# One kernel of two layers: in the first layer's step loop, TensorE multiplies weights and values ahead of the first banks of exponents and scores

## The chip, the core and the metric

The kernel runs on one core of a Trainium2 chip. A core has five engines with their own instruction queues: TensorE (PE; its weight loads are PEld), VectorE (DVE), ScalarE (ACT), GpSimd (POOL) and SyncE (SP, which issues the DMAs here). They meet through semaphores only. Matrix products land in PSUM, which has 8 banks of 128 partitions x 512 fp32 values; TensorE may write a bank again once the engine that reads it has signalled. The metric is the device time of one execution in microseconds, the median of several.

## The reference

Two transformer layers over x of shape 4 x 512 x 512, fp32. Each is an attention and a feed-forward part, each with a LayerNorm ahead of and behind it and a residual:

```python
x = x + _layernorm(_L0_attn_ref(_layernorm(x, axis=-1), L0_attn_Wq, L0_attn_Wkv, L0_attn_Wo), axis=-1)
x = x + _layernorm(_L0_ffn_ref(_layernorm(x, axis=-1), L0_ffn_q_scales, L0_ffn_q_vals, L0_ffn_bias), axis=-1)
x = x + _layernorm(_L1_attn_ref(...), axis=-1)
x = x + _layernorm(_L1_ffn_ref(...), axis=-1)
```

The change lies in the first attention: 32 heads of 16 columns, one key and value head for all, a linear position bias and a causal mask.

```python
scores = jnp.einsum('bqhd,bkd->bhqk', q, k) * scale
scores = jnp.where(causal[None, None], scores + bias[None], -jnp.inf)
attn = jax.nn.softmax(scores, axis=-1)
out = jnp.einsum('bhqk,bkd->bqhd', attn, v).reshape(b, s, h)
return out @ Wo
```

The first feed-forward part is one product with dequantized weights and a bias. The second layer (grouped attention with rotary positions, then a gated octonion feed-forward) isn't touched.

## The kernel before

Every fp32 operand of a product is split into two fp16 tensors, `hi` and `lo`, and three products (hi x hi, lo x hi, hi x lo) are added in PSUM.

The first layer (`layer0`) is one loop of steps, n from -6 to 73, written out once for each engine. A step works on pairs of heads; there are 64 pairs (4 batches x 16), and a pair passes through several steps:

- Step n: the scores of pair n (`scores`), in five banks s0 to s4, only for their row maxima. VectorE reduces each bank (`maximise`, L1074 for banks 0 and 1, L1076 for 2 and 3, L1079 for 4). The maxima of four pairs are joined, transposed, and put back by DMA as rows of `q_stack`.
- Step n: the exponents of pair n - 6 (`exponents`), transposed, with maxima subtracted, in five banks x0 to x4. ScalarE takes the exponential of each bank (`exponential`, L872). GpSimd casts them to hi in three pieces (`weights_hi`, L564) and makes the last piece's lo (L566); VectorE makes the other lo halves, two pieces, one step later (`weights_lo`, L1088).
- Step n: the product of weights and values of pair n - 8 (`weigh_values`, 60 matmuls of 17 columns into one bank, L687 and L690). ScalarE copies the heads out (`copy_heads`, L879), VectorE takes reciprocals, GpSimd normalises.
- Between these, `others(n)` puts in queries (q), keys (K), values (V), the products of output (y) and feed-forward (f), and transposes of normed rows (n1, n2, n3) and heads (o). The first of a step's others stands between bank 2 and 3, a large one in two halves about bank 3; the rest and the transpose of maxima (m) stand between bank 3 and 4.

The banks are in three groups (`groups`): three for scores, two for exponents, three for the rest, each used in turn. Before a bank is filled, `take` waits until the filling that used it before has been emptied. So the third-last filling of the last group (PV, others, m) must be emptied before PV can start; a transpose is emptied by VectorE's lo half (`lo4`, L1019), after ScalarE's hi half (L823).

The queues are strict in the order written. ScalarE's steps also carry the row norms (L863) between the exponentials in some steps (of 16: steps 0, 4, 8, 10 and 14, where a batch has them). VectorE's step: lo half 0 of pair n - 7, maxima 0 and 1, lo half 1, maxima 2 and 3, first other, statistics, maximum 4, other others, reciprocals.

Of the kernel before, what the change touches and what calls it, by code (L numbers as in the profile page):

```python
# [213 lines left out]
def layer0(nc, A, W0, C, K0, N1, xT, x2_dram):  # L214
# [9 lines left out]
    with ExitStack() as stack:  # L224
# [138 lines left out]
        def others(n):  # L363
            out = []
            g, r = divmod(n + 5, GP)
            if r == 0 and 0 <= g < NG:
                out.append(("q", g))
            if at(n, FRONT["K"]) is not None:
                out.append(("K", at(n, FRONT["K"])))
            for kind in ("y", "f"):  # L370
                out += [(kind, b, t) for t in range(TT) for b in range(B)
                        if n == PAIRS * b + offset(kind, b, t) and has(kind, b)]
            if at(n, FRONT["V"]) is not None:
                out.append(("V", at(n, FRONT["V"])))
            for kind, when in (("n1", FRONT["n1"]), ("n2", BACK["n2"]), ("n3", BACK["n3"])):
                for i, w in enumerate(when):
                    b = at(n, w)
                    if b is not None and has(kind, b):
                        out += [(kind, b, 2 * i), (kind, b, 2 * i + 1)]
            out += [("o", b, t) for t in range(TT) for b in range(B) if n == PAIRS * b + offset("o", b, t)]  # L380
            return out
# [78 lines left out]
        with nc.Block() as block:  # L460
# [158 lines left out]
            def _(pe):  # L619
# [29 lines left out]
                def scores(p, i):  # L649
                    g, pp = p // GP, p % GP  # L650
                    if (pp, i) == (0, 0):
                        pe.wait_ge(s_qs[g % 2], 16 * 6 * (g // 2 + 1))
                        pe.wait_ge(s_kr, 4 * (g // GP) + 2)
                    out = take(("s", p, i))
                    for e, t, c in PARTS[i]:
                        w = P * (t + 1)
                        pe.matmul(out[:, c:c + w], qs[:, g % GP, pp, t * P:(t + 1) * P], kz[:, g // GP % 2, e, 0:w],  # L657
                                  start=True, stop=False)
                        ins = pe.matmul(out[:, c + w - P:c + w], far[:, :], tri[:, :], start=False, stop=True)
                    ins.then_inc(s_sf, 1)  # L660

                def exponents(p, i):
                    g, pp = p // GP, p % GP
                    if (pp, i) == (0, 0):
                        pe.wait_ge(s_mr[g % 2], 16 * 4 * (g // 2 + 1))
                        pe.wait_ge(s_kr, 4 * (g // GP) + 4)
                    out = take(("x", p, i))
                    for e, j, c in XPARTS[i]:
                        pe.matmul(out[:, c:c + S - j * P], ks[:, g // GP % 2, e, j * P:(j + 1) * P],  # L669
                                  qs[:, g % GP, pp, j * P:S], start=True, stop=False)  # L670
                        ins = pe.matmul(out[:, c:c + P], far[:, :], trit[:, :], start=False, stop=True)  # L671
                    ins.then_inc(s_ef, 1)
# [22 lines left out]
                def turn_maxima(g):  # L695
                    out = take(("m", g))
                    pe.wait_ge(s_mx, g + 1)
                    pe.transpose(out[:, 0:P], mx[:, g % 2, :], C["ident"][:, :]).then_inc(s_mf, 1)
# [70 lines left out]
                def turn(n, *which):  # L769
                    for i in which:  # L770
                        if 0 <= n - X_LAG < NP:
                            exponents(n - X_LAG, i)
                        if 0 <= n < NP:
                            scores(n, i)

                for n in STEPS:
                    extra = others(n)
                    if n == 0:
                        pe.wait_ge(s_sc, 1)
                    turn(n, 0, 1)  # L780
                    if 0 <= n - V_LAG < NP:
                        weigh_values(n - V_LAG)
                    turn(n, 2)
                    split = bool(extra) and extra[0][0] in ("K", "q", "y", "f")
                    for u in extra[:1]:
                        if split:
                            half(u, 0)
                        else:
                            fill(u)
                    turn(n, 3)  # L790
                    for u in extra[:1]:
                        if split:
                            half(u, 1)
                    if n % GP == 0 and 0 <= n // GP - 1 < NG:
                        turn_maxima(n // GP - 1)
                    for u in extra[1:]:
                        fill(u)
                    turn(n, 4)
# [1987 lines left out]
```

## Time and profile before

| | |
|---|---|
| median of 3 runs | 2198.66 us (2198.51 to 2199.24) |
| the profiled execution's own time | 2201.45 us |
| its span, first to last instruction | 2199.3 us |
| mean granted TensorE clock | 0.978 |
| busy TensorE / VectorE / ScalarE / GpSimd | 2061.8 / 1755.3 / 1387.8 / 950.2 us |
| first layer's step loop | about 62 to 640 us; x banks from 95 to 577 us |

The page gives the engine, the line in the kernel, the tile names, and the microseconds of each. A wait is put down to the engine that released it last. Matmuls overlap, so a matmul's duration is longer than its distance to the next one; in the timelines the distance between starts counts. "PEclk" is the share of TensorE's full clock that was granted.

### The profile page before, as it was taken

The page shows a single profiled execution, that of the slowest core. Times are in us where ns is not written, and L with a number is a line of the kernel's source. Part 1 is how long each engine was busy: PE and PEld are TensorE (multiplying, and loading weights), DVE is VectorE, ACT ScalarE, POOL GpSimd, SP SyncE. Part 2 cuts the span into 40 slices and gives each one's busy share as a digit, 9 for nine tenths or more (in the row PEclk, how much of TensorE's full clock was granted, in tenths as well). Part 3 has the DMA queues.
Part 4 walks back from the last instruction along what each step waited for, and adds up shares of the span by engine and source line. Part 5 has one row for each costly group of instructions (what it writes and reads, how often), then busy time and mean ns, then how long its engine had stood idle before and what let it go on. Part 6 is the DMA issues. An engine that isn't in the chain of part 4 may idle for free. (4 is left out here: it accounts for less than half of the span.)

```text
span 2199.3 us, 48564 instructions
## 1 busy us (share of the span) xinstructions
PE 2061.8 (94%) x18563; PEld 1248.1 (57%) x18563; DVE 1755.3 (80%) x3692; ACT 1387.8 (63%) x3037; POOL 950.2 (43%) x902
## 2 busy tenths in 40 slices
PE   8798999898878899999999999999999999888998
PEld 3466666666434556656566565666666665534443
DVE  5799899998766787778878778777877877967665
ACT  3466665666456777777777777767777876661221
POOL 0188798879743323233333332332333323253221
PEclk9899999999879999999999999999999999999999
DMA  6110101101122453354354354444354443420001
GB/s 240 47 36 17 55 17 48 36 18 41 44 96 55 92 101 76 71 95 92 63 97 90 67 93 89 71 91 92 63 99 80 73 89 76 98 71 27 32 20 39
DMA packets 390214, 153.81 MB, mean 70 GB/s; under 512 B 358544, under 2 KB 369424, under 8 KB 387936
## 3 DMA queue, kind: packets, MB, share of 16 engines
q1 hardware_dynamic: 389984, 150.71, 31.5%
q8 instruction: 148, 2.42, 0.5%
q14 instruction: 82, 0.67, 0.1%
HBM read 48.69 MB, written 11.53 MB: 27 GB/s over the span
## 5 line engine op out<-in xcount | busy, mean ns | idle before, releaser
L1899 POOL TENSOR_TENSOR q_in_sbuf<-q_in_sbuf,sinq 128x512 f32<-128x512 f32 x128 | 162.6, 1271 | 720.1 <-ACT q_in_sbuf L2031 598.5
L2043 ACT ACTIVATE xp<-xp,nm 128x128 f32<-128x128 f32 (+3 forms) x512 | 281.3, 550 | 199.0 <-DVE nm L2126 199.0
L1925 PE MATMUL bank<-xT_hi,weights_and_hi 128*128 128x512 f16 x1280 | 383.0, 381 | 7.0 <-DVE yacc L2141 3.8
L872 ACT ACTIVATE weights_and_hi<-bank,unit 128x512 f32<-128x512 f32 x320 | 213.4, 687 | 152.3 <-PE bank L671 149.6
L2008 ACT ACTIVATE probs_hi<-xp,rl 128x128 f16<-128x128 f32 (+3 forms) x512 | 245.1, 550 | 68.2 <-DVE rl L2146 64.4
L2095 DVE SCALAR_TENSOR_TENSOR probs_lo<-xp,rl,probs_hi 128x128 f16<-128x128 f32 (+3 forms) x512 | 282.4, 612 | 0.0
L2103 DVE TENSOR_TENSOR q1T_lo<-qf,q1T_hi 128x512 f16<-128x512 f32 x128 | 88.4, 691 | 222.8 <-ACT q1T_hi L2022 222.8
L2126 DVE CUSTOM_DVE_ANT_0 xp<-bank,mask,cs 128x128 f32<-128x128 f32 (+3 forms) x512 | 250.3, 545 | 0.0
L1925 PE MATMUL bank<-xT_lo,weights_and_hi 128*128 128x512 f16 x640 | 243.6, 381 | 0.0
L564 POOL CAST weights_and_hi<-weights_and_hi 128x1024 f16<-128x1024 f32 (+1 forms) x192 | 198.4, 1053 | 85.9 <-ACT weights_and_hi L872 85.4
L1925 PE MATMUL bank<-p1T_hi,v_hi 128*128 128x128 f16 x1280 | 221.0, 219 | 2.6 <-DMA p1T_lo<-probs_lo 2.6
L1925 PE MATMUL bank<-p1T_hi,v_lo 128*128 128x128 f16 x1280 | 221.0, 219 | 0.0
L1925 PE MATMUL bank<-p1T_lo,v_hi 128*128 128x128 f16 x1280 | 221.0, 219 | 0.0
L1925 PEld LDWEIGHTS bank<-xT_hi,weights_and_hi 128*128 128x128 f16 x1280 | 124.7, 98 | 161.0 <-issue 15.0
L1906 POOL TENSOR_TENSOR qf<-q_in_sbuf,t 128x512 f32<-128x512 f32 x160 | 203.9, 1274 | 12.7 <-POOL q_in_sbuf L1899 0.2
L1925 PE MATMUL bank<-wo_hi,o1T_hi 128*128 128x512 f16 x512 | 195.0, 381 | 6.3 <-DVE wo_lo L2185 4.7
L1925 PE MATMUL bank<-wo_hi,o1T_lo 128*128 128x512 f16 x512 | 195.1, 381 | 0.0
L1925 PE MATMUL bank<-wo_lo,o1T_hi 128*128 128x512 f16 x512 | 195.1, 381 | 0.0
L1088 DVE TENSOR_TENSOR weights_lo<-weights_and_hi 128x1024 f16<-128x1024 f32 x128 | 181.4, 1421 | 6.0 <-POOL weights_and_hi L564 6.0
L657 PE MATMUL bank<-k_stack_max,q_stack 128*128 128x512 f16 (+3 forms) x512 | 137.2, 310 | 32.2 <-DVE mx L1076 12.9
L1925 PE MATMUL bank<-kT_hi,q1T_hi 128*128 128x128 f16 (+3 forms) x512 | 148.1, 302 | 11.0 <-DVE q1T_lo L2103 8.3
L669 PE MATMUL bank<-q_stack,k_stack 128*128 128x512 f16 (+3 forms) x512 | 139.1, 313 | 17.2 <-ACT weights_and_hi L872 10.0
(311 smaller groups left out, 5498.2 us busy)
## 6 DMA issues: line engine op xcount, KB each, us to landing
weights_and_hi<-in_wq SPq DMA_DIRECT2D x8, 1024.0 KB, 6.0
raw_o<-in_wo SPq DMA_DIRECT2D x8, 1024.0 KB, 6.0
x_front<-in_x SPq DMA_DIRECT2D x5, 1024.0 KB, 6.1
q_stack<-q_hi SPq DMA_DIRECT2D x64, 64.0 KB, 2.6
wup<-in_wup SPq DMA_DIRECT2D x3, 1024.0 KB, 11.9
fused_scratch<-weights_and_hi SPq DMA_DIRECT2D x12, 256.0 KB, 2.5
xb<-in_x SPq DMA_DIRECT2D x3, 1024.0 KB, 5.2
x_scratch<-xb SPq DMA_DIRECT2D x3, 1024.0 KB, 4.3
```

The lines of the kernel that those rows point to most:

```text
L564: pool.tensor_copy(ph[0][:, p % 2, c0:c1, :], px[:, p % 2, c0:c1, :]).then_inc(s_wh, 1)
L657: pe.matmul(out[:, c:c + w], qs[:, g % GP, pp, t * P:(t + 1) * P], kz[:, g // GP % 2, e, 0:w], start=True, stop=False)
L669: pe.matmul(out[:, c:c + S - j * P], ks[:, g // GP % 2, e, j * P:(j + 1) * P], qs[:, g % GP, pp, j * P:S], start=True, stop=False)
L872: act.activation(px[:, p % 2, i, :], bank_of(("x", p, i))[:, :], ACT.Exp, scale=unit[:, 0:1]).then_inc(s_ed, 1)
L1088: dve.tensor_tensor(ph[1][:, p % 2, c, :], px[:, p % 2, c, :], ph[0][:, p % 2, c, :], ALU.subtract).then_inc(s_wl, 1)
L1899: pool.tensor_tensor(qs[:, i % 2, :], qs[:, i % 2, :], rope["sink" if u[0] == "k" else "sinq"][:, :], ALU.mult).then_inc(s_rot, 1)
L1906: pool.tensor_tensor(qf[:, i % 2, :], qs[:, i % 2, :], t2[:, i % 2, :], ALU.add).then_inc(s_qf, 1)
L1925: ins = pe.matmul(out, lhs(a), rhs(c), start=(first and i == 0), stop=(last and i == 2))
L2008: ins = act.activation(pr[0][:, m % 2, c], xp[:, m % 3, c], ACT.Copy, scale=rl[:, m % 3, t:t + 1])
L2043: ins = act.activation(x, x, ACT.Exp, scale=-1.0, bias=nm[:, m % 3, t:t + 1], accum_out=ls[:, m % 3, t:t + 1])
L2095: ins = dve.scalar_tensor_tensor(pr[1][:, m % 2, c], xp[:, m % 3, c], rl[:, m % 3, t:t + 1], pr[0][:, m % 2, c], ALU.mult, ALU.subtract)
L2126: ins = dve.tensor_tensor_reduce(out=xp[:, m % 3, TRI[t]:TRI[t] + w], in0=bank_of(("s", m, i))[:, col:col + w], in1=mask[:, S - w:S], scal ...
```

## The change

In TensorE's block, the call of `weigh_values` moves ahead of the banks 0 and 1 of exponents and scores. No other engine's code changes.

```diff
                     if n == 0:
                         pe.wait_ge(s_sc, 1)
-                    turn(n, 0, 1)
                     if 0 <= n - V_LAG < NP:
                         weigh_values(n - V_LAG)
-                    turn(n, 2)
+                    turn(n, 0, 1, 2)
                     split = bool(extra) and extra[0][0] in ("K", "q", "y", "f")
```

TensorE, head of step 26, before. The rows from `q_stack,k_stack` are exponents, those from `k_stack_max,q_stack` scores, those with `v` the product of pair 18; brackets name the semaphores waited for (`s_t_lo_out`: VectorE's lo halves of transposes):

```order
L657 MATMUL bank<-k_stack_max,q_stack 128x256
...
L669 MATMUL bank<-q_stack,k_stack 128x512 [waits s_exponentials,s_key_stacks_ready,s_maxima_stacked1]
...
L657 MATMUL bank<-k_stack_max,q_stack 128x512 [waits s_scores_maximised]
...
L669 MATMUL bank<-q_stack,k_stack 128x512 [waits s_exponentials]
...
L657 MATMUL bank<-k_stack_max,q_stack 128x512 [waits s_scores_maximised]
...
L687 MATMUL bank<-v,weights_and_hi 128x17 [waits s_last_weights_lo,s_weights_lo,s_t_lo_out]
...
L669 MATMUL bank<-q_stack,k_stack 128x384 [waits s_exponentials]
...
L657 MATMUL bank<-k_stack_max,q_stack 128x128 [waits s_scores_maximised]
```

The same place after:

```order
L657 MATMUL bank<-k_stack_max,q_stack 128x256 [waits s_scores_maximised]
...
L687 MATMUL bank<-v,weights_and_hi 128x17 [waits s_last_weights_lo,s_weights_lo,s_t_lo_out]
...
L669 MATMUL bank<-q_stack,k_stack 128x512 [waits s_exponentials,s_key_stacks_ready,s_maxima_stacked1]
...
L657 MATMUL bank<-k_stack_max,q_stack 128x512 [waits s_scores_maximised]
...
L669 MATMUL bank<-q_stack,k_stack 128x512 [waits s_exponentials]
...
L657 MATMUL bank<-k_stack_max,q_stack 128x512 [waits s_scores_maximised]
...
L669 MATMUL bank<-q_stack,k_stack 128x384 [waits s_exponentials]
```

The product's group of 60 matmuls, with its three waits, stands ahead of x0; x0, s0, x1, s1 and x2 follow in their old order.

TensorE, head of step 69, before (exponents of pair 63, product of pair 61; there are no scores any more):

```order
L669 MATMUL bank<-q_stack,k_stack 128x256 [waits s_exponentials]
...
L669 MATMUL bank<-q_stack,k_stack 128x512 [waits s_exponentials]
...
L669 MATMUL bank<-q_stack,k_stack 128x512 [waits s_exponentials]
...
L687 MATMUL bank<-v,weights_and_hi 128x17 [waits s_last_weights_lo,s_weights_lo,s_pv_out]
...
L669 MATMUL bank<-q_stack,k_stack 128x384 [waits s_exponentials]
...
L639 MATMUL bank<-wf_hi,back_T_hi 128x512 [waits s_t_lo_out]
```

The same place after:

```order
L669 MATMUL bank<-q_stack,k_stack 128x256 [waits s_exponentials]
...
L687 MATMUL bank<-v,weights_and_hi 128x17 [waits s_last_weights_lo,s_weights_lo,s_pv_out]
...
L669 MATMUL bank<-q_stack,k_stack 128x512 [waits s_exponentials]
...
L669 MATMUL bank<-q_stack,k_stack 128x512 [waits s_exponentials]
...
L669 MATMUL bank<-q_stack,k_stack 128x384 [waits s_exponentials]
...
L639 MATMUL bank<-wf_hi,back_T_hi 128x512 [waits s_t_lo_out]
```

There x0 and x1 of the last pair moved behind the product, which waits for GpSimd's lo half (`s_last_weights_lo`).

## Rows read from the trace of the kernel before

**Rows 1.** Busy time (x instructions) by engine, PEclk, DMA share, GB/s, by stretch.
```profile
100.00:230.00 130.00, 117.22 (x1908) 85.21 (x1906) 128.14 (x197) 84.52 (x153) 113.36 (x102) 1.00 0.08 25
...
530.00:590.00 60.00, 48.81 (x693) 33.45 (x692) 43.88 (x58) 33.65 (x63) 51.22 (x48) 0.80 0.16 45
```

**Rows 2.** What VectorE waited for, 230 to 530 us: us in total, times, longest.
```profile
DVE mx L1079 <- PE bank L659: 8.6, 6, 1.8
DVE st L1005 <- ACT ya L853: 4.2, 7, 1.3
```

**Rows 3.** What TensorE's weight loads waited for, 100 to 530 us.
```profile
PEld bank L657 <- DVE mx L1076: 23.2, 38, 2.3
PEld bank L669 <- ACT weights_and_hi L872: 19.3, 41, 1.4
...
PEld bank L687 <- DVE front_T_lo L1019: 1.6, 4, 0.5
```

**Rows 4.** TensorE's timeline, step 26: start us, us, instruction, [idle before <-releaser].
```profile
227.59 0.38 PE L669 MATMUL bank<-q_stack,k_stack 128*128 128x512 f16 x1
...
229.24 0.21 PE L687 MATMUL bank<-v,weights_and_hi 128*128 128x17 f16 x2 [0.15 <-DVE front_T_lo L1019]
...
230.76 0.32 PE L669 MATMUL bank<-q_stack,k_stack 128*128 128x384 f16 x1
```

**Rows 5.** Timeline of VectorE, steps 26 and 27.
```profile
228.51 0.68 DVE L1019 TENSOR_TENSOR front_T_lo<-bank,front_T_hi 128x512 f16<-128x512 f32 x1
...
245.61 0.69 DVE L1079 TENSOR_REDUCE mx<-bank 128x2 f32<-128x512 f32 x1 [1.77 <-PE bank L659]
```

**Rows 6.** Timeline of TensorE, step 11.
```profile
127.58 0.39 PE L657 MATMUL bank<-k_stack_max,q_stack 128*128 128x512 f16 x1 [0.90 <-DVE mx L1076]
...
127.86 0.38 PE L669 MATMUL bank<-q_stack,k_stack 128*128 128x512 f16 x1
...
129.97 0.32 PE L669 MATMUL bank<-q_stack,k_stack 128*128 128x384 f16 x1
```

**Rows 7.** Timeline of VectorE, step 11.
```profile
125.71 1.21 DVE L1088 TENSOR_TENSOR weights_lo<-weights_and_hi 128x1024 f16<-128x1024 f32 x1
```

**Rows 8.** Timeline of ScalarE, step 11.
```profile
128.33 0.69 ACT L872 ACTIVATE weights_and_hi<-bank,unit 128x512 f32<-128x512 f32 x1 [0.87 <-PE bank L671]
```

**Rows 9.** Timeline of TensorE, step 59.
```profile
494.79 0.39 PE L669 MATMUL bank<-q_stack,k_stack 128*128 128x512 f16 x1 [0.85 <-ACT weights_and_hi L872]
...
496.86 0.32 PE L669 MATMUL bank<-q_stack,k_stack 128*128 128x384 f16 x1
```

**Rows 10.** Timeline of ScalarE, end of step 58 and head of step 59.
```profile
494.06 0.67 ACT L872 ACTIVATE weights_and_hi<-bank,unit 128x512 f32<-128x512 f32 x1
494.63 0.81 ACT L863 ACTIVATE yb<-yb,nb,rs 128x512 f32<-128x512 f32 x1
```

**Rows 11.** Busy time by engine, from step 55 on.
```profile
462.00:472.50 10.50, 10.50 (x124) 6.56 (x122) 8.28 (x13) 5.03 (x9) 5.15 (x5) 1.00 0.01 2
```

**Rows 12.** Timeline of TensorE, step 53.
```profile
447.52 0.21 PE L687 MATMUL bank<-v,weights_and_hi 128*128 128x17 f16 x2
```

**Rows 13.** Timeline of VectorE, steps 53 and 55.
```profile
446.79 0.68 DVE L1019 TENSOR_TENSOR back_T_lo<-bank,back_T_hi 128x512 f16<-128x512 f32 x1
...
472.31 0.69 DVE L1079 TENSOR_REDUCE mx<-bank 128x2 f32<-128x512 f32 x1 [1.78 <-PE bank L659]
```

**Rows 14.** Timeline of TensorE, step 69.
```profile
569.97 0.20 PE L687 MATMUL bank<-v,weights_and_hi 128*128 128x17 f16 x2 [0.41 <-POOL weights_lo L566]
```

**Rows 15.** Timeline of GpSimd, step 69.
```profile
567.81 2.01 POOL L566 TENSOR_TENSOR weights_lo<-weights_and_hi 128x512 f16<-128x512 f32 x1
```

**Rows 16.** Timeline of VectorE, step 69.
```profile
576.61 0.75 DVE L1060 SCALAR_TENSOR_TENSOR yb<-bank,gm,bias 128x512 f32<-128x512 f32 x1 [1.72 <-PE bank L639]
```

**Rows 17.** VectorE's lo half of the weights: count, shortest, median and longest in ns.
```profile
L1088 DVE TENSOR_TENSOR weights_lo<-weights_and_hi x128: 1165/1215/2316, 103.2 to 581.5; 128x1024 f16<-128x1024 f32 x128
```

**Rows 18.** Granted clock (PEclk, after POOL) in steps 34 and 35.
```profile
297.00:303.00 6.00, 5.93 (x85) 3.73 (x83) 5.86 (x14) 1.64 (x4) 5.92 (x7) 0.72 0.01 3
```

## The prediction

> **What bounds the kernel now.** I read the page's slices first, then the busy time by stretch, the waits of each engine, and last the timeline of single steps. The change touches only the step loop of the first layer, which puts its first exponent bank at 95 us and its last product of weights and values at 585 us. Between 100 and 230 us VectorE is busy 128.1 of 130 us [rows 1], which leaves 1.9 us for all its waits. Its own instructions set the pace there. Between 230 and 530 us it waits 19.7 us, of which 8.6 for scores from TensorE and 4.2 for ScalarE copies of output banks that TensorE fills late [rows 2], the rest mostly for such copies of queries, keys and transposes. In those places TensorE is the bound. Steps with an output or query product are TensorE's, the others VectorE's. TensorE waits often, mostly at the head of a step: 23.2 us for the maxima that free score banks, 19.3 for exponentials [rows 3]. For weights and values ("PV" below) it waits only 1.6 us, behind a lo half of a transposed tile [rows 3]. From 530 us GpSimd sets the pace, busy 51.2 of 60 us [rows 1].
>
> **What the change does to a step.** A step n fills x0 s0 x1 s1 PV x2 s2 x3 s3 x4 s4 (x: exponents, s: scores), with other products between. Now PV stands ahead of x0. Nothing is added or removed: 60 short matmuls move past four banks, 64 times. No DMA and no instruction of another engine moves. PV takes 1.52 us (229.24 to 230.76, rows 4), the four banks 0.28 us each when nothing is late (127.58 to 127.86, rows 6), 1.12 us together.
>
> PV needs three things. (a) The weights of pair n-8: VectorE's second lo half, which it computes just ahead of the maximum that s0 waits for. In step 11 that half ends at 125.71 + 1.21 = 126.92, while s0 goes at 127.58 [rows 6, 7]. (b) GpSimd's last lo half of the pair: by the timeline of every step from 8 to 63 it is done before the head, but for step 35, where it is 0.06 us late. (c) A bank of the group of three that is filled for PV, transposes and products in turn. After a step with three other fillings that bank is the first of them, and it is emptied late in VectorE's step. In step 26 its lo half ends at 228.51 + 0.68 = 229.19 and PV starts at 229.24; x0, s0, x1, s1 had run meanwhile from 227.59 [rows 4, 5]. I read (c) from the timeline of each step: it already holds PV back in steps 9, 25, 26, 37, 42 and 53, and it comes 1.15 us after the head in steps 41 and 49.
>
> **Price A, where (c) ends last.** PV starts as before, but four banks now stand behind it, so x2 comes at least 1.12 us later. ScalarE adds to that: an exponential starts 0.47 us after its bank's matmul (127.86 to 128.33), lasts 0.69, and the bank is taken 0.06 us later (494.06 + 0.67 to 494.79): 1.22 us from x0 to x2 [rows 6, 8 to 10]. I take 1.22. The ends are 0 (the wait is passed on to nothing) and 1.22 plus ScalarE's queue behind the late exponentials, 0.8 us for one row norm (494.63, rows 10).
> - Step 26: x2 moves from 230.76 to 231.98 and TensorE is dense on to 245.6, where VectorE waits 1.77 us for scores [rows 4, 5]. But step 27 wins 0.2 at x1, and steps 28 to 31, still TensorE's, 0.6 together. 1.2 - 0.2 - 0.6 = +0.4.
> - Step 53: PV starts at 447.52, right after back_T_lo (446.79 + 0.68). TensorE is busy 10.50 of the last 10.5 us up to VectorE's next long wait, 1.78 us at 472.31 [rows 11 to 13], and as dense in the 12 us ahead of these. All of it arrives: +1.25.
> - Steps 37 and 38: the lateness meets a score wait in step 39 (0.66 us of gap), so about +0.4. Step 42: +1.2, of which step 43 gives 1.0 back: +0.2.
> - Steps 9, 25, 41, 49: the third score bank waits for VectorE's maximum anyway, and the maxima of banks 3 and 4 start 1.4 to 1.8 us after these could. Zero; the cover is VectorE's dense queue.
> - The tail: PV of pair 61 (the last is 63) waits for GpSimd's lo half (567.81 + 2.01 = 569.82) and starts at 569.97; x2 follows 1.5 us later, then products for which VectorE waits 1.72 us at 576.61 [rows 14 to 16]. x0 and x1 now stand between: +1.2.
>
> **Price B, ScalarE.** In steps 24, 36, 40 and 52, whose row norms sit between the exponentials, exponentials 0 and 1 come about 1.3 us later and push copies of transposes. VectorE reads one 0.3 us too early in perhaps three: +0.9.
>
> **Gain C, where the head waited for something else.**
> - Steps bound by the score bank: in step 11 PV can run from 126.97 to 128.48, x2 comes at 129.70 instead of 129.97 [rows 6, 7]. That is 0.27 us, and it counts only where VectorE waits afterwards: three such steps in the dense stretch, -0.8 (at most the 1.9 us of idle time there, rows 1).
> - Step 59: x1 waited until 494.79 for the last exponential of the step before. With PV at 493.23 to 494.74, x2 is bound by ScalarE's norm (to 495.44) and exponential 0, about 496.06 instead of 496.86: -0.8, and step 58 gives 0.3 more [rows 9, 10]. Together -1.1.
> - Step 62, -0.4. In other steps (18, 22, 33, 34, 47) the head's wait is covered too, but the next one, for VectorE's maximum or ScalarE, ends as before: zero.
>
> **The sum.** 0.4 + 1.25 + 0.4 + 0.2 + 1.2 + 0.9 - 0.8 - 1.1 - 0.4 = +2.05 us. The profiled span of 2199.3 would become 2201.3. Its run took 2201.45 us, 2.8 above the median of 2198.66, so I add the 2.05 to the median: **2200.7 us**.
>
> **A second look at GpSimd.** One lo half of VectorE takes 1.165 to 2.316 us, 128 of them [rows 17]; their total on the page's line is 181.4 us, mean 1.42, so 32 us lie above the shortest. The long ones overlap GpSimd's two-input operations. Later first exponentials could shift GpSimd's casts, but it starts a pair's first cast 1.3 us or more after its exponential in nearly all steps, and the later casts hang on x3 and x4. I take 0, with 3 us to either side (a tenth of the 32). The Trainium skill (SBUF — State Buffer, "Who interferes with whom") says that a VectorE instruction with two SBUF inputs and a GpSimd instruction that reads SBUF contend, and that whichever starts first blocks the other. The trace agrees on the lengthening; by that rule a shift of either sign could cost as much as it saves, and the sum would stay.
>
> **Rivals.**
> 1. *PV at the head blocks the banks behind it everywhere (slower).* Against my zeros: all eight steps of price A pay 1.22 us, and the tail. 9 x 1.22 = 11.0, less C's 2.3, plus B's 0.9: +9.6, 2208. It decides once the maxima's slack of 1.4 to 1.8 us after a late s3 is used up, for instance by the ScalarE queue's 0.8 us on top of 1.22 (2.0 in all). For: TensorE is in order. Against: VectorE is dense in these steps. A half of it is +5, 2204.
> 2. *The head waits are simply filled (faster).* TensorE waits 42.5 us for maxima and exponentials [rows 3]; if a third of VectorE's 19.7 us went, with the tail's price halved: about -6, 2193. Against: (a) opens only 0.66 us ahead of s0, and (c) is a wait that filling can't shorten.
> 3. *TensorE's clock.* After two waits of 1.9 and 1.5 us in steps 34 and 35 the granted clock was 0.72 over six us [rows 18], that is partly at 1.2 instead of 2.4 GHz; 28% of six us is 1.7 us lost. There are three such drops between 290 and 525 us. Moving PV closes some gaps (step 35's, ahead of s0) and joins others into one of up to 2.1 us (step 37). One drop more or fewer: 2202.4 or 2199.0. The Trainium skill (TensorE: Matmul & The Clock Gate, "What's actually happening") says that the default state is throttled and activity releases it, which speaks for a drop more wherever a joined gap lengthens. The profile has gaps of 1.5 us without a drop, so the sum leaves it out.
> 4. *No change* (PV hides wholly): 2198.7, inside my range.
>
> **Chances.** What a measurement here can tell from no change is about 0.2%, 4.4 us: 2194.3 to 2203.1. My forecast with 3 and 4: 0.62, of which 0.06 ends above 2203.1 and 0.01 below 2194.3. Rival 1, whole or half: 0.25, of which 0.05 still lies within. Rival 2: 0.13, of which 0.04 within. Faster 0.10, same 0.64, slower 0.26. Range: 2195.5 (half of rival 2, or 3 us from GpSimd) to 2207 (most of rival 1).
>
> **What would show it.** In the new profile: PV starts at the head in most steps, and after a front_T_lo or back_T_lo in steps 26, 37, 42 and 53 at an unchanged distance from it; TensorE waits of 0.3 us or less for exponentials at x2; VectorE's waits between 230 and 530 us near 20 us; the stage's last PV near 586 to 587 us; then everything shifted by one constant. I am wrong if the step loop to 530 us is over 3 us longer or shorter, if maxima of banks 3 or 4 are waited for in steps 9, 25, 41 and 49, or if the mean of VectorE's lo half moves by more than 0.03 us.

## The result, and the profile after

| kernel | median | lowest to highest | executions |
|---|---|---|---|
| before | 2199.64 us | 2198.40 to 2202.01 | 13 |
| after | 2204.44 us | 2203.02 to 2209.69 | 13 |

By the medians the change costs 4.8 us. The ratio, which is estimated from all executions, is 1.0028, with a 95% interval of 1.0020 to 1.0035, which is 6.2 us (4.4 to 7.7). It is not the quotient of the medians, here and below; the two agree within the interval. The forecast was 2200.7, range 2195.5 to 2207.0. The sign and the range held; the size was too small by more than half. The profiled execution of after is its longest, 2209.69 us with a span of 2207.6. The same kernel, run and profiled once more, gave 2206.14 us with a span of 2204.0. I call it "after, second" and read terms from it where a typical execution is wanted. Lines behind 779 have a number one lower than before. A "fall" of the clock is a stretch in which PEclk is 0.50 instead of 1.00.

Busy time by stretch of after, columns as in [rows 1]. The second row is the whole stretch from 230 to 530 us, the last one the 7 us behind step 26's wait:

```profile
100.00:230.00 130.00, 116.91 (x1891) 84.43 (x1890) 128.18 (x196) 82.94 (x149) 111.03 (x102) 0.99 0.08 25
230.00:530.00 300.00, 277.04 (x3901) 190.08 (x3898) 274.40 (x443) 177.44 (x314) 239.13 (x223) 0.95 0.11 34
530.00:590.00 60.00, 47.97 (x701) 33.57 (x698) 41.94 (x62) 39.65 (x71) 55.22 (x52) 0.76 0.07 20
229.00:236.00 7.00, 6.86 (x90) 4.59 (x91) 6.69 (x10) 2.76 (x6) 3.60 (x4) 0.76 0.08 25
```

The same stretches of before, those that [rows 1] lack:

```profile
230.00:530.00 300.00, 276.58 (x4008) 191.29 (x4005) 278.87 (x457) 183.07 (x325) 248.47 (x230) 0.98 0.11 34
229.00:236.00 7.00, 6.85 (x102) 4.63 (x100) 7.00 (x12) 4.02 (x8) 4.81 (x4) 1.00 0.10 31
```

From 230 to 530 us TensorE is as busy as before (277.0 to 276.6 us) and does fewer instructions (3901 to 4008). Its granted clock is 0.95 instead of 0.98. VectorE is busy 4.5 us less, since it does less in the same time. That TensorE is as busy as before is easy to misread: a slow TensorE looks as busy as a fast one, and only PEclk and the counts tell them apart.

What VectorE waited for, 230 to 530 us of after (us in total, times, longest), against [rows 2]:

```profile
DVE mx L1078 <- PE bank L659: 8.7, 6, 1.8
DVE st L1004 <- ACT ya L852: 4.8, 7, 1.3
DVE q_lo L1050 <- ACT q_hi L846: 3.9, 5, 1.2
DVE k_placed L1027 <- ACT k_hi L833: 1.2, 1, 1.2
DVE mx L1073 <- PE bank L659: 1.2, 4, 0.5
DVE mx L1075 <- PE bank L659: 1.2, 2, 0.8
```

In all VectorE waits 23.7 us there, 19.7 before.

What TensorE's weight loads waited for, 100 to 530 us of after, against [rows 3]:

```profile
PEld bank L669 <- ACT weights_and_hi L871: 19.0, 52, 1.7
PEld bank L657 <- DVE mx L1073: 13.7, 15, 3.3
PEld bank L687 <- issue: 12.2, 15, 1.9
...
PEld bank L687 <- DVE front_T_lo L1018: 4.6, 4, 1.5
PEld bank L687 <- DVE back_T_lo L1018: 2.9, 2, 1.4
PEld bank L687 <- DVE m_lo L1097: 2.5, 2, 1.3
```

Before has this row besides those in [rows 3]:

```profile
PEld bank L657 <- DVE mx L1074: 14.0, 22, 2.3
```

The waits for maxima of banks 0 to 3 shrank from 23.2 + 14.0 us to 13.7. The product of weights and values (L687) took the waiting over: where before had 1.6 us for a front_T_lo and 0.7 for a back_T_lo, after has 4.6 + 2.9 + 2.5 us for lo halves of the rest group, in pieces of up to 1.5 us, and 12.2 us for no releaser that the profile shows.

TensorE in step 26 of after (start us, us, instruction, [idle before <-releaser]), against [rows 4]:

```profile
229.14 0.21 PE L687 MATMUL bank<-v,weights_and_hi 128*128 128x17 f16 x2 [1.15 <-DVE front_T_lo L1018]
...
230.66 0.42 PE L669 MATMUL bank<-q_stack,k_stack 128*128 128x512 f16 x1
...
231.51 0.63 PE L669 MATMUL bank<-q_stack,k_stack 128*128 128x512 f16 x1
...
232.58 0.53 PE L669 MATMUL bank<-q_stack,k_stack 128*128 128x384 f16 x1
```

PV starts behind front_T_lo as before, now after one wait of 1.15 us. x0, x1 and x2 follow at 230.66, 231.51 and 232.58. The second 128x512 matmul lasts 0.63 us where one of before lasts 0.38, and x1 to x2 takes 1.07 us where two banks took 0.56. From the granted clock, 0.76 over the seven microseconds, half the clock (1.2 instead of 2.4 GHz) was granted for a part of them. x2 moved by 1.82 us, and VectorE's first maximum of step 27 lies 2.71 us more behind before's than that of step 26.

Step 9 has the same form; the forecast had it at zero. TensorE's row there in after:

```profile
114.23 0.21 PE L687 MATMUL bank<-v,weights_and_hi 128*128 128x17 f16 x2 [1.25 <-DVE front_T_lo L1018]
```

And in before:

```profile
115.52 0.21 PE L687 MATMUL bank<-v,weights_and_hi 128*128 128x17 f16 x2 [0.15 <-DVE front_T_lo L1019]
```

In the tail this profile agrees with the forecast. GpSimd's last lo half, PV and VectorE's wait in step 69 of after, against [rows 14 to 16]:

```profile
577.22 2.01 POOL L566 TENSOR_TENSOR weights_lo<-weights_and_hi 128x512 f16<-128x512 f32 x1
```
```profile
579.37 0.20 PE L687 MATMUL bank<-v,weights_and_hi 128*128 128x17 f16 x2 [0.49 <-POOL weights_lo L566]
```
```profile
587.29 0.75 DVE L1059 SCALAR_TENSOR_TENSOR yb<-bank,gm,bias 128x512 f32<-128x512 f32 x1 [3.00 <-PE bank L639]
```

PV comes 9.40 us later than before (579.37 to 569.97), VectorE's feed-forward row 10.68 (587.29 to 576.61): the tail adds 1.28 us. VectorE's lo half, against [rows 17], kept its mean (181.5 us in 128, 1.42 each):

```profile
L1087 DVE TENSOR_TENSOR weights_lo<-weights_and_hi x128: 1164/1234/2307, 101.9 to 592.2; 128x1024 f16<-128x1024 f32 x128
```

**How the traces are compared.** The start of VectorE's first maximum in each step is a good ruler, since all kernels have it 64 times. Its shift against before grows or shrinks at the steps where time is lost or won. For after, second:

| first maximum of step | change of the shift, us | edit or cause |
|---|---|---|
| 9 and 10 | +0.39, +1.06 | steps 8 and 9 |
| 12, 14, 17, 20 | -0.13, -0.15, -0.14, -0.13 | gain C |
| 25, 41, 53 | +0.24, +0.30, +0.24 | price B |
| 27, then to 32 | +2.71, then -0.34 | step 26 |
| 38 | +1.33 | step 37 |
| 43, 44 | +0.96, -0.28 | step 42, given back in 43 |
| 49, 50 | +0.93, -0.55 | steps 48 and 49 |
| 54, 55 | +0.82, +0.28 | step 53 |
| 59, 60, 61 | -0.15, -1.24, +0.68 | steps 58 and 59 |

From step 8 to 63 all terms make +7.3 us (ahead of step 8 the executions already differ by up to 1.3 us, without any edit), and the tail adds 1.3. In the first profile it is +10.6 us.

What the loop and its tail lose doesn't arrive whole. The next layer's first ScalarE copy of queries starts 10.8 us later than before in the first profile and 7.4 us later in the second, but the executions end 8.3 and 4.7 us later. The second layer from there on, with no instruction changed, took 2.5 and 2.7 us less than in the profile of before, and in the profiles of the experiments 0.1 to 3.7 us less. So a shift of a few microseconds in one profile isn't the change of a median; terms are read from the first maxima, costs from the medians.

### The profile page after: what moved, and what is told of

The parts are those of the page before. It is cut to its first block and busy times, and to the rows that moved or that the text cites. A ratio compares the mean times of both kernels' runs of the same rounds, so it can differ in the third digit from the quotient of the medians.

```text
span 2207.6 us, 48564 instructions
## 1 busy us (share of the span) xinstructions
PE 2070.8 (94%) x18563; PEld 1253.3 (57%) x18563; DVE 1758.0 (80%) x3692; ACT 1389.1 (63%) x3037; POOL 946.7 (43%) x902
## 5 line engine op out<-in xcount | busy, mean ns | idle before, releaser
L1087 DVE TENSOR_TENSOR weights_lo<-weights_and_hi 128x1024 f16<-128x1024 f32 x128 | 181.5, 1422 | 5.1 <-POOL weights_and_hi L564 5.1
L1924 PE MATMUL bank<-kT_lo,q1T_hi 128*128 128x128 f16 (+3 forms) x512 | 154.5, 302 | 0.0
## 6 DMA issues: line engine op xcount, KB each, us to landing
wup<-in_wup SPq DMA_DIRECT2D x3, 1024.0 KB, 11.9
```

Of the source, the lines that this page charges most:

```text
L1087: dve.tensor_tensor(ph[1][:, p % 2, c, :], px[:, p % 2, c, :], ph[0][:, p % 2, c, :], ALU.subtract).then_inc(s_wl, 1)
L1924: ins = pe.matmul(out, lhs(a), rhs(c), start=(first and i == 0), stop=(last and i == 2))
```

## The experiments

All ran against the kernel before on the same chip; times are medians with the lowest and highest. "Late steps" are the eight in which the bank of the rest group ends last: 9, 25, 26, 37, 41, 42, 49 and 53. In the texts on record theory L says that the late bank, with the clock, makes the cost; theory S, that ScalarE's queue (price B) makes it all over the loop.

**After, second.** No edit.

> The changed kernel again, on the chip of the three others. Theory L (late bank: the loss comes from the eight steps 9, 25, 26, 37, 41, 42, 49 and 53, whose PV waits for a bank, and from the granted clock that falls in that joined wait): +4 to +6 us over before, with two groups of runs, some 3 us apart, by how many times the clock falls; in the profile at least five falls of the clock before 535 us, against three before the change. Theory S (ScalarE: exponentials 0 and 1 come later in every step and delay its copies): the same +4 to +6, but the clock's falls are a by-product and don't decide a run's time.

2206.14 us (2204.96 to 2208.03), before 2198.24; ratio 1.0034 (1.0021 to 1.0047). That is +7.9 us by the medians, above the +4 to +6 of both theories, though the interval reaches down to 4.6. The five executions don't form two groups. The falls did come: seven of them between 100 and 535 us, against three in before. Its step loop loses time at the same places as the first profile, to 0.1 us each up to step 51. From there the first profile lost 3.1 us more, with further falls of the clock at 435 and 456 us.

**The new order except in the late steps and the tail.** `turn(n, 0, 1)` stands ahead of `weigh_values` where `head` is false, `turn(n, 2)` behind it:

```diff
+                    head = n < NP and n not in (9, 25, 26, 37, 41, 42, 49, 53)
+                    if not head:
+                        turn(n, 0, 1)
                     if 0 <= n - V_LAG < NP:
                         weigh_values(n - V_LAG)
-                    turn(n, 0, 1, 2)
+                    turn(n, 2) if not head else turn(n, 0, 1, 2)
```

> PV at the head in all steps from 8 to 63 but the eight with a late bank (9, 25, 26, 37, 41, 42, 49, 53) and the steps from 64 on, which keep the old order. Theory L: only the gains of price C and price B are left, +0.9 - 2.3 us, so before -1.4, between -2.5 and 0. Theory S: nearly all steps are still changed, so +3 to +5 us. The tail (steps from 64 on) is out too: were it the tail alone, this would be -1.4 as well, and the run with the eight steps alone would be 0.

2198.62 us (2195.61 to 2201.48), ratio 1.0001 (0.9992 to 1.0010). The whole cost is gone, so the late steps and the tail make it. Theory S asked for +3 to +5 us and is out, since the interval ends at +2.2. The forecast gain of 1.4 us did not show.

**The new order in the late steps only.**

Against the edit above:

```diff
-                    head = n < NP and n not in (9, 25, 26, 37, 41, 42, 49, 53)
+                    head = n in (9, 25, 26, 37, 41, 42, 49, 53)
```

> PV at the head only in the eight steps with a late bank, the old order in all others. Theory L: prices of these steps without the gains elsewhere, which feed on the same waits: +5 to +8 us, above the changed kernel. Theory S: 8 of 56 steps, under +1 us. Tail alone: 0.

2209.24 us (2207.01 to 2211.40), ratio 1.0046 (1.0034 to 1.0059). By the medians (+11.0 us, more than the +5 to +8 expected) eight steps cost more than the whole change does, and the rest of the change gives some back; the intervals of the two ratios overlap.

**Late steps kept busy.** The order of after, and in the late steps four spare products into x0's bank, which x0 overwrites, run while PV's bank is waited for:

```diff
+                    if n in (9, 25, 26, 37, 41, 42, 49, 53):
+                        spare = take(("x", n - X_LAG, 0))
+                        for _ in range(4):
+                            pe.matmul(spare[:, :], far[:, :], posr[:, :], start=True, stop=True)
```

> The changed kernel, with four matmuls of 128 x 512 ahead of PV in each of the eight steps, into the free bank that x0 takes next and overwrites (0.86 us of work in a wait of 1.2 to 1.9 us). If the granted clock is part of the loss (theory L): faster than the changed kernel by 1 to 3 us, that is before +2 to +3, with the runs closer together, and one or two falls of the clock fewer in each place; the 1.22 us a step of banks behind PV stay. If the clock is no part: the same as the changed kernel or up to 1 us slower.

2201.69 us (2198.98 to 2204.50), ratio 1.0014 (1.0005 to 1.0023). TensorE has more work, and the time is 4.4 us less than after, second, on the same chip. The slowest of these eleven executions is faster than the fastest of those five. The text on record expected them closer together; they spread over 5.5 us, the five over 3.1. Step 26 on TensorE: the spare products, PV, x0 and x2.

```profile
227.09 1.03 PE L783 MATMUL bank<-position_rows,far 128*128 128x512 f16 x4
...
228.41 0.21 PE L687 MATMUL bank<-v,weights_and_hi 128*128 128x17 f16 x2 [0.29 <-DVE front_T_lo L1022]
...
229.93 0.38 PE L669 MATMUL bank<-q_stack,k_stack 128*128 128x512 f16 x1
...
231.20 0.34 PE L669 MATMUL bank<-q_stack,k_stack 128*128 128x384 f16 x1
```

The granted clock behind it, in the same kernel:

```profile
228.00:235.00 7.00, 6.69 (x97) 4.33 (x97) 7.00 (x11) 3.50 (x7) 4.41 (x5) 1.00 0.10 31
```

The idle piece is 0.29 us instead of 1.15, the clock stays at 1.00, and x0 to x2 takes 1.27 us. So the order alone delays x2 by what the forecast said, and the rest of step 26 went away with the fall behind it. The first maxima tell the same (us):

| change of the shift at | 10 | 27 | 38 | 43 |
|---|---|---|---|---|
| after, second | +1.06 | +2.71 | +1.33 | +0.96 |
| kept busy | +0.46 | +1.25 | +0.35 | +0.44 |
| clock's part | 0.60 | 1.46 | 0.98 | 0.52 |

Together 3.6 us. After, second has falls at 114.7, 230.8, 316.1 and 353.7 us, right behind the waits for PV's bank in steps 9, 26, 37 and 41; with TensorE kept busy none of the four is left. The last stands behind step 41's wait of 1.04 us, so the 0.52 us at step 43 is not step 42's own:

```profile
353.20 0.21 PE L687 MATMUL bank<-v,weights_and_hi 128*128 128x17 f16 x2 [1.04 <-DVE m_lo L1097]
```

**Four late steps.** `head = n in (26, 37, 42, 53)`.

> The order of before everywhere, but in steps 26, 37, 42 and 53 the product of weights and values stands ahead of x0. Theory L (late bank and clock): these four steps alone give +4 to +6 us against before. From the maxima of the kernel with the new order everywhere: 2.7 at step 26, 1.35 at 37, 0.95 at 42 and 0.8 to 2.6 at 53, less the 0.3 to 0.5 us that dense steps give back between them; the granted clock falls behind each of the four. Theory P (the prediction's price A as it was written, no clock): 0.4 + 0.4 + 0.2 + 1.25 = +2.2 us. If the cost sits in the sum of many steps instead: under +1.

2206.82 us (2205.99 to 2211.35), before 2199.65; ratio 1.0039 (1.0027 to 1.0052): +7.2 us by the medians, above both theories. Its first maxima rise by 2.43, 1.82, 1.92 and 1.07 us behind the four steps, and by 1.19 at step 36 and 1.50 at step 63, where no instruction changed. Behind step 35's old wait the clock now lost 3.4 us, in before 1.7. All kernels that have the old order and no spare products in steps 34 and 35 fit this: the four that lose 3.4 us there pay 1.19 or 1.20 us at step 36, the five that lose 1.7 or nothing pay nothing. Step 53's rise has no fall behind it.

**The other four.** `head = n in (9, 25, 41, 49)`.

> The order of before everywhere, but in steps 9, 25, 41 and 49 the product stands ahead of x0. The prediction said zero for these four: 0, within 0.5 us. The trace of the kernel after says otherwise for step 9: its first maximum came 1.47 us later, with a fall of the granted clock behind the joined wait, and steps 25 and 41 gave 0.25 to 0.3 each: +1.3 to +2.0 us for the four.

2203.62 us (2201.72 to 2207.71), ratio 1.0019 (1.0010 to 1.0028): +4.0 us, more than the +1.3 to +2.0 expected. The four steps themselves: +1.61 (step 9), +0.34 (25), +0.40 (41), and +0.51 and -0.52 about step 49. The rest are again unchanged places: +1.20 at step 36, +0.51 at 44, +1.56 and -0.51 at 52 and 53, +1.70 at 63.

**The tail alone.** `head = n >= NP`.

> The order of before in all steps up to 63, and the product ahead of x0 from step 64 on. The prediction's price for the tail: +1.2 us (+0.1 to +1.5 by the start of layer 1 in the kernels run so far), no shift of any maximum before 525 us. If the tail hides it: 0.

2199.64 us (2196.66 to 2202.79), ratio 1.0003 (0.9994 to 1.0012). No cost is measured, but the interval (-1.3 to +2.6 us) doesn't exclude the forecast +1.2. Its first maxima lie 0.1 to 0.5 us ahead of before's at every step. The next layer's first ScalarE copy of queries starts at 646.04 us, in before at 646.28. With the first maximum of step 63 0.44 us ahead, the tail adds 0.2 us. Over the same stretch the six kernels with the old tail and no spare products lie between -0.66 and +0.08, so the price is 0.1 to 0.9 us. From PV to the feed-forward row, the ruler that gave 1.28 in after, the tail alone adds 0.59.

**Spare products in the waits, in the order of before.** Six in step 61 ahead of s3, three in step 62 ahead of s0, and more ahead of PV in the last steps:

```diff
+                def spend(bank, count):
+                    for _ in range(count):
+                        pe.matmul(bank[:, :], far[:, :], posr[:, :], start=True, stop=True)
...
+                    if n in (67, 68, 69):
+                        spend(take(("pv", n - V_LAG)), 2 if n == 69 else 6)
...
-                    turn(n, 3)
+                    if n == 61:
+                        exponents(n - X_LAG, 3)
+                        spend(take(("x", n - X_LAG, 4)), 6)
+                        scores(n, 3)
+                    else:
+                        turn(n, 3)
```

> The order of before, with spare products of 128x512 (operands far and posr) put where TensorE waits anyway: six into x4's bank in step 61, three into x1's bank in step 62, six into the output bank of weights and values in steps 67 and 68, four and two in step 69. Each is overwritten by the first real product of its bank. If the granted clock falls in these waits and costs time (the clock part of theory L): -1 to -2.5 us against before. If the clock in the last steps of the stage decides nothing, or the spare products delay what stands behind them: 0 to +1 us.

2196.75 us (2194.61 to 2199.21), ratio 0.9988 (0.9979 to 0.9996): 2.9 us less than before by the medians, a little more than expected. The first maximum of step 63 gains 0.76 us on that of step 62.

**Four late steps kept busy.** The kernel with `head = n in (26, 37, 42, 53)`, and the four spare products in these steps:

```diff
                     if not head:
                         turn(n, 0, 1)
+                    else:
+                        spare = take(("x", n - X_LAG, 0))
+                        for _ in range(4):
+                            pe.matmul(spare[:, :], far[:, :], posr[:, :], start=True, stop=True)
```

> As the kernel with the product ahead of x0 in steps 26, 37, 42 and 53 only, but in these four steps four spare products of 128x512 run into x0's bank while the product's bank is waited for; x0 overwrites them. If the falls of the granted clock behind the joined waits are most of the +7.2 us that the four steps cost: +2 to +3.5 us against before (price A as the prediction had it is +2.25; the first maxima of the kernel with spare products in all late steps give 1.25 + 0.35 + 0.44 + 0.82 = 2.9). If the cost is the order of the banks alone: +6 to +8 us still.

2207.66 us (2202.96 to 2209.35), before 2199.29; ratio 1.0028 (1.0016 to 1.0041). The total is a miss: +8.4 us by the medians, by the interval 3.5 to 9.0, where the clock theory asked for 2 to 3.5. The spare products did not lower the +7.2 us of the same four steps without them, so this run doesn't bear the theory out as a whole. Two of the four steps did as expected: step 26 cost 1.25 instead of 2.43, step 42 cost 0.44 instead of 1.92. Step 53 cost 1.07 instead of 1.06; it had no fall to lose. In step 37 the spare products ran too early, PV still waited in one piece, and the cost stayed at 1.82 us:

```profile
314.48 0.21 PE L687 MATMUL bank<-v,weights_and_hi 128*128 128x17 f16 x2 [0.95 <-DVE back_T_lo L1025]
```

The kernel with all late steps kept busy waited 0.35 us there. In places where no instruction changed the profile pays another 1.20 (step 36), 1.49 (48) and 1.50 us (63).

**Ten chosen steps.** The order of before, PV ahead of x0 only where earlier kernels had won time:

```diff
+                    early = n in (11, 13, 16, 19, 27, 29, 31, 43, 58, 59)
+                    if early:
+                        weigh_values(n - V_LAG)
                     turn(n, 0, 1)
-                    if 0 <= n - V_LAG < NP:
+                    if not early and 0 <= n - V_LAG < NP:
```

> The order of before, with the product ahead of x0 only in steps 11, 13, 16, 19, 27, 29, 31, 43, 58 and 59, whose next first maximum came earlier in the kernels run so far: 0.10 to 0.16 us each in eight of them, 0.79 in step 43, 1.23 in step 59. Gains that add up: -3 us against before. If these gains come back as waits further down (GpSimd sets the pace from 530 us on): 0 to -1.

2198.50 us (2195.04 to 2200.63), ratio 0.9995 (0.9986 to 1.0004): -0.8 us by the medians, as the second of the two expectations had it. In its trace the gains are there: -0.11 to -0.17 in eight places, -0.78 at step 44, -1.24 at step 60. But it pays 1.19 us at step 36 and 1.63 at step 48, and step 61 takes 0.66 back.

**Ten chosen steps and the spare products of steps 61 to 69.** Both edits.

> The kernel with the product ahead of x0 in the ten chosen steps, and the spare products in steps 61, 62, 67, 68 and 69. The spare products alone gave -2.9 us. If both add: -4.5 to -6 us against before, the best of all. If the end of the stage is set by GpSimd and takes the chosen steps' gain back: -3, as with the spare products alone.

2197.42 us, ratio 0.9989 (0.9979 to 0.9998), with ten of eleven executions from 2192.36 to 2201.16: 1.9 us under before by the medians, less than either expectation, though the interval reaches to -4.6. The eleventh took 3502.65 us, with a mean granted clock of 0.556 against 0.98 in the others; it has no trace, and its cause is open. Up to step 60 this kernel and the one ahead have the same instructions in the same order. In the profiled executions their first maxima of step 54 still lie 3.7 us apart, 0.6 of it from ahead of step 8. The wait ahead of x1 in step 47 and the 7 us behind it in the kernel without spare products:

```profile
398.24 0.39 PE L669 MATMUL bank<-q_stack,k_stack 128*128 128x512 f16 x1 [1.03 <-ACT weights_and_hi L875]
```
```profile
399.00:406.00 7.00, 6.83 (x86) 4.20 (x83) 5.92 (x13) 4.80 (x9) 6.35 (x7) 0.76 0.47 152
```

The same in the kernel with them:

```profile
396.57 0.39 PE L669 MATMUL bank<-q_stack,k_stack 128*128 128x512 f16 x1 [1.03 <-ACT weights_and_hi L896]
```
```profile
397.00:404.00 7.00, 6.83 (x102) 5.01 (x100) 6.33 (x14) 5.82 (x11) 6.65 (x8) 1.00 0.52 152
```

The same instruction waits the same 1.03 us. In one execution TensorE then gets 0.76 of its clock and does 86 instructions, in the other 1.00 and 102. The waits of 1.77 and 1.36 us in steps 34 and 35 differ in the same way: behind them the granted clock over six us is 0.64 in the one and 1.00 in the other. So a wait of over a microsecond is a risk and not a fixed price. Nor is the length of the wait all that counts: before waits 1.57 and 2.00 us in one piece ahead of 414.6 and 432.0 us with no fall behind, after in step 41 1.04 us with one.

**More spare products.** As the kernel ahead, and also:

```diff
-                    if n == 62:
+                    if n in (35, 50, 51, 62):
                         exponents(n - X_LAG, 0)
-                        spend(take(("x", n - X_LAG, 1)), 3)
+                        spend(take(("x", n - X_LAG, 1)), {35: 4, 50: 4, 51: 5, 62: 3}[n])
                         scores(n, 0)
                         turn(n, 1)
+                    elif n == 47:
+                        turn(n, 0)
+                        spend(take(("pv", n - V_LAG)), 3)
+                        turn(n, 1)
...
-                    if n == 61:
+                    if n in (34, 61):
```

> The kernel with the ten chosen steps and the spare products of steps 61 to 69, and further spare products of 128x512 in the regular waits behind which the granted clock fell in some executions and not in others: six ahead of s3 in step 34, four ahead of s0 in step 35, three ahead of x1 in step 47, four ahead of s0 in step 50 and five in step 51. If these chance falls are what makes executions of one kernel differ by several us: no fall between 100 and 540 us, a first maximum of step 63 at -4 us or earlier, a median 4 to 6 us under before, and a spread of the executions under 4 us (7.8 us for before in the last comparison). If the falls there have little to do with the spread: -2 us as without these spare products, and the same spread.

2192.86 us (2192.03 to 2194.21), before 2197.95 (2194.82 to 2202.38); ratio 0.9977 (0.9967 to 0.9986). This is 5.1 us under before, the best of all, and its ten executions lie within 2.2 us, those of before within 7.6. All its numbers came as the first theory said. (The text above gives 7.8 us for the spread of before in the comparison ahead of this one; on record it is 9.8.) TensorE in steps 34 and 35, and the clock:

```profile
291.73 0.23 PE L657 MATMUL bank<-k_stack_max,q_stack 128*128 128x128 f16 x1 [0.48 <-DVE mx L1102]
...
293.40 1.04 PE L778 MATMUL bank<-position_rows,far 128*128 128x512 f16 x4 [0.24 <-ACT weights_and_hi L900]
```
```profile
100.00:540.00 440.00, 408.40 (x6125) 284.89 (x6124) 419.34 (x670) 280.16 (x501) 374.98 (x343) 1.00 0.10 33
```

**All kernels side by side.** "Clock lost" adds up what PEclk lacks to 1 in each microsecond from 100 to 540 us of the profiled execution; the shift is that of the first maximum of step 63 against before, and the last column leaves out what was there at step 8 already.

| kernel | clock lost, us | shift, us | from step 8 on |
|---|---|---|---|
| before | 5.4 | 0 | 0 |
| chosen steps and more spare products | 0.0 | -4.4 | -3.4 |
| chosen steps and spare products | 1.7 | -4.1 | -3.2 |
| order of before, spare products | 1.7 | -1.1 | -0.9 |
| tail alone | 3.4 | -0.4 | 0.0 |
| chosen steps | 10.3 | +0.3 | +0.5 |
| new order except in late steps | 10.5 | -0.3 | +0.9 |
| after, late steps kept busy | 6.8 | +1.4 | +2.6 |
| after, second | 15.4 | +6.1 | +7.3 |
| four other late steps | 15.4 | +6.7 | +7.0 |
| four late steps kept busy | 13.6 | +8.3 | +9.5 |
| after | 18.8 | +9.3 | +10.6 |
| late steps only | 11.9 | +9.5 | +9.9 |
| four late steps | 15.4 | +10.6 | +10.8 |

The two go together but are not proportional. I read this as falls that count only where TensorE sets the pace. Before itself loses 1.7 us at 298 us and the tail-only kernel does not, with no difference in the maxima behind it. The first two kernels below before lie close together because the profile of the one with one fall is of its fastest execution, 2192.36 us; by the medians they are 5.1 and 1.9 us under before.

## Why the prediction was right or wrong

- **The range** held, but not for the sum's reasons: it reached to 2207 for rival 1, and no term of the sum was the clock.
- **What bounds the kernel** held in the main: VectorE's waits for the maxima of bank 4 stay what they were (8.7 to 8.6 us), its waits in all grew from 19.7 to 23.7, and the cost sits where TensorE sets the pace.
- **Price A, as an order.** Right in size but for step 26. x0 to x2 was put at 1.22 us; with TensorE kept busy it was 1.27. Without the clock's part step 26 costs 1.25 less the 0.35 that steps 27 to 31 give back (forecast +0.4, so 0.5 too little), step 37 +0.35 (+0.4), step 42 +0.44 - 0.27 (+0.2), step 53 +0.82 (+1.25). The next 0.28, at step 55, can't be laid to step 53: the kernel that keeps its old order has it too.
- **The step that failed** is rival 3's last sentence, "so the sum leaves it out". I had seen that the change joins gaps, and took the falls of the clock as one more or one fewer. There were some eight more (1.7 us of full clock each): the clock lost from 100 to 540 us rose from 5.4 to 18.8 us, in after, second to 15.4, six more. Their part at four places is 3.6 us by the kernel kept busy, more than the 2.75 us between the forecast of +2.05 and the measured +4.8. In the loop alone the forecast's terms add up to +0.85 from step 8 on; after, second has +7.3, with TensorE kept busy +2.6. So most of what was missing went away with the falls, and 1.8 us is order that the terms had too small.
- **Why its argument failed.** It was that the profile has gaps of 1.5 us without a drop. That is true and proves only that a gap is no certain drop. I had counted the three drops, but not how many gaps of over a microsecond the change would add. In after PV's bank makes one of 1.04 to 1.25 us in six of the eight late steps (9, 26, 37, 41, 49 and 53) and shorter ones in 25 and 42 (0.86 and 0.48). Where a microsecond lies wholly within a fall, PEclk is 0.50, outside 1.00. The Trainium skill (TensorE: Matmul & The Clock Gate, "What's actually happening") has just these two levels as well. It also says that the count of slow matmuls varies between runs of one kernel. It says so of a kernel's start; the pair of executions above shows the like in the middle of one.
- **Zero for steps 9, 25, 41, 49** was wrong for step 9: +1.06 at once and +1.61 with this group alone, each with a joined wait (1.25 and 2.07 us) and a fall behind it. With TensorE kept busy it is +0.46. The others cost 0.1 to 0.4. The cover, VectorE's dense queue, holds for most of the 1.2 us of order but not for half the clock on top of it.
- **The tail**, +1.2: 1.28 in after, 1.26 in after, second, but 0.59 by the same ruler when it is changed alone, and then nothing that the median shows. Why it costs less there stays open; the shift of the loop ahead of it differs.
- **Price B**, +0.9: 0.24 to 0.30 at steps 25, 41 and 53, also in the kernel without the late steps, 0.8 together. There were more of this kind that I had not listed, 0.25 at step 9 and 0.39 at step 49 and, in the kernel without the late steps, 0.29 at step 54. Step 36's row norm, whose price would stand at step 37, showed none.
- **Gain C**: steps 11, 13, 16 and 19 gave 0.55 together (-0.8 forecast), steps 58 and 59 gave 1.39 (-1.1). Then 0.67 came back at step 61, also in the kernel with ten chosen steps (0.66), which I had not seen. Step 43's -0.79 is the part that the forecast counted against step 42. Step 62 (-0.4) gave 0.64 in the kernel kept busy; in after, where the clock lost 3.4 us at 520 us instead of 1.7, the shift grew by 0.22 to 0.52.
- **Rival 1** asked for 1.22 us in every late step and was put at +5 for its half. The number fits after; the mechanism does not, since it leaves out the clock and the zeros mostly held as an order. **Rival 2** did not come. Its 42.5 us of waits left out the 14.0 us for the maxima of banks 0 and 1; they shrank as it said, but the waits for PV grew. **GpSimd** as forecast: the mean of VectorE's lo half moved by less than 0.01 us.
- **What I said would show me wrong** did: the loop to 530 us is more than 3 us longer (+9.3; +6.1 in after, second). The other signs did not fire: no maximum of banks 3 or 4 is waited for in steps 9, 25, 41 and 49 (those of banks 0 or 1 are, up to 0.46 us, in 9, 41 and 49). The last product of the stage starts at 593.7 us (590.5) and not at 586 to 587, and what follows isn't shifted by one constant.

Settled by experiments: that the late steps make the cost, and that spare products in all eight take most of it away (4.4 us of 7.9), with the four falls that stood there. Not settled: why the same in four steps didn't lower the median. Its profile has falls at places whose instructions didn't change and pays for them there. Only argued: how much of the median is due to such falls, since a profile shows one execution. That they follow from where the waits lie in time was not tested by itself. The 0.51 us at step 44 in four kernels whose step 43 is unchanged is unexplained, and so is the second layer's difference of up to 3.7 us.

## What to carry to other kernels

Before work is moved ahead on TensorE, list the waits it will meet in one piece, and price each of about a microsecond or more with a possible fall of the granted clock, in steps where TensorE sets the pace. An order that spreads a wait over several short ones is worth keeping even if each product then stands later than it could. Where a long wait can't be avoided, spare products that run into a bank which the next real product overwrites can fill it, if they last until the wait ends: with 31 of them in the step loop and 18 in its tail, and PV moved only in ten steps where the trace had shown a gain, the kernel came to 2192.86 us against 2197.95, and the spread of its executions shrank from 7.6 to 2.2 us.

## What the hardware showed that I had not expected

- Behind equal waits of 1.03 us, and of 1.77 and 1.36 us, in equal code, the granted clock was 0.76 and 0.64 in one execution and 1.00 in another.
- A fall costs VectorE's queue between nothing (at 298 us of before) and 1.6 us (step 48 of the kernel with ten chosen steps).
- A change of a few steps moved falls in others: four kernels with unchanged steps 34 and 35 paid 1.2 us behind them (1.19, 1.20, 1.20, 1.19), where the clock lost 3.4 us; before, which lost 1.7 us there, and four kernels without a fall there paid nothing.
- One execution of eleven, of a kernel whose others took 2192 to 2201 us, took 3502.65 us at a mean granted clock of 0.556.
- The executions of before spread over 3.6 to 9.8 us in five comparisons; those of the kernel without a fall in its step loop over 2.2 us.
